# Where the value products stand and which banks they fill, in a transformer tower on one core

## The reference

```python
def _stablemax3_s(x):
    pos = 1.0 + x * (1.0 + 0.5 * x * (1.0 + x / 3.0))
    neg = 1.0 / (1.0 - x * (1.0 - 0.5 * x * (1.0 - x / 3.0)))
    return jnp.where(x >= 0, pos, neg)
# logits - max; s / sum(s)
attn = stablemax3(einsum('bhsd,bhtd->bhst', q, k) * scale)
out = einsum('bhst,bhtd->bhsd', attn, v)
h = h + out @ w_out.T + b_out
hid = relu(einsum('bsd,edf->bsef', layernorm(h), W1) + b1)
y = einsum('bsef,efd->bsed', hid, W2) + b2     # 4 experts, mixed per token
```

## Time and profile before

| | |
|---|---|
| median of 3 runs | 4353.31 us (4352.80 to 4353.53) |
| profiled execution, its own time | 4351.56 us |
| its span in the trace | 4349.7 us |
| PE busy | 4268.4 us (98%), 21312 instructions |
| DVE busy | 2292.8 us (53%) |
| ACT busy | 2174.9 us (50%) |
| HBM traffic | 14 GB/s over the span |

### The profile page before, as it was taken

One profiled execution on the slowest core, in us unless ns is written; L12 is line 12 of the kernel. 1 busy time (PEld: TensorE's weight loads), 2 busy tenths in 40 slices (PEclk: granted clock), 3 DMA queues, 4 the chain that ended last, 5 costly groups with the idle time before them and its releaser, 6 DMA issues.

```text
span 4349.7 us, 53831 instructions
## 1 busy us (share of the span) xinstructions
PE 4268.4 (98%) x21312; PEld 2342.4 (54%) x21312; DVE 2292.8 (53%) x3334; ACT 2174.9 (50%) x2945; POOL 141.4 (3%) x141
## 2 busy tenths in 40 slices
PE   6799999999999999999999999999999999999999
PEld 3455555555555555555555555555555555555555
DVE  4555555555555555555555555555555555555542
ACT  4444555445555445554455554455544555544552
POOL 1000000000000000000000000000000000000000
PEclk8899999999999999999999999999999999999999
DMA  3000000000000000000000000000000000000000
GB/s 129 12 3 14 16 16 16 16 1 16 16 16 16 3 14 16 16 16 16 1 16 16 16 16 3 14 16 16 16 16 1 16 16 16 16 3 14 4 5 8
DMA packets 29991, 65.61 MB, mean 15 GB/s; under 512 B 5360, under 2 KB 20400, under 8 KB 28720
## 3 DMA queue, kind: packets, MB, share of 16 engines
q1 hardware_dynamic: 26720, 62.07, 4.2%
q10 hardware_dynamic: 3024, 0.09, 0.0%
HBM read 49.24 MB, written 12.91 MB: 14 GB/s over the span
## 4 chain that ended last, share of the span: by engine, by line
PE 93%; DVE 4%; ACT 1%; issue 1%; POOL 0%; DMA 0%; DVEq 0%; SPq 0%; ACTq 0%; POOLq 0%
PE ps L697 32%; PE ps L708 30%; PE ps L763 6%; PE ps L732 5%; PE ps L745 4%; PE ps L720 4%; PE ps L802 4%; PE ps L811 2%; PE ps L819 2%; PE ps L687 1%; DVE probs L485 1%; DVE xn L536 1%; PE ps L788 1%; PE ps L794 1%; PE ps L776 0%
## 5 line engine op out<-in xcount | busy, mean ns | idle before, releaser
L697 PE MATMUL ps<-xn,w1s 128*128 128x394 f32 x4096 | 1562.8, 505 | 0.0
L708 PE MATMUL ps<-hT,w2s 128*128 128x394 f32 x4096 | 1535.0, 497 | 0.1
L416 ACT ACTIVATE hT<-ps,b1s 128x394 f32<-128x394 f32 x1024 | 605.3, 591 | 1400.9 <-PE ps L697 1400.9
L697 PEld LDWEIGHTS ps<-xn,w1s 128*128 128x128 f32 x4096 | 745.6, 190 | 628.4 <-issue 185.0
L708 PEld LDWEIGHTS ps<-hT,w2s 128*128 128x128 f32 x4096 | 756.1, 189 | 553.6 <-issue 35.4
L485 DVE SCALAR_TENSOR_TENSOR probs<-probs,ps 99x788 f32<-99x788 f32 x512 | 476.0, 971 | 657.5 <-ACT probs L320 657.5
L554 DVE TENSOR_REDUCE lows<-ps 99x8 f32<-99x1576 f32 x256 | 459.6, 1797 | 367.7 <-PE ps L732 367.5
L325 ACT ACTIVATE probs<-probs 99x1576 f32<-99x1576 f32 x256 | 388.4, 1517 | 194.0 <-DVE probs L485 194.0
L320 ACT ACTIVATE probs<-ps 99x788 f32<-99x788 f32 x512 | 395.5, 826 | 147.3 <-PE ps L720 145.4
L329 ACT ACTIVATE probs<-probs 99x1576 f32<-99x1576 f32 x256 | 387.1, 1512 | 0.0
L763 PE MATMUL ps<-x,wtok 128*128 128x392 f32 x744 | 256.3, 492 | 0.0
(11 more groups left out here) (82 smaller groups left out, 2502.9 us busy)
## 6 DMA issues: line engine op xcount, KB each, us to landing
x<-in_xT SPq DMA_DIRECT2D x31, 1188.0 KB, 5.6
out_rows<-rows SPq DMA_DIRECT2D x64, 99.0 KB
out_rows<-rows SPq DMA_DIRECT2D x64, 98.0 KB
w1s<-in_w SPq DMA_DIRECT2D x4, 1024.0 KB, 13.2
w2s<-in_w SPq DMA_DIRECT2D x4, 1024.0 KB, 15.1
x<-in_xT SPq DMA_DIRECT2D x6, 198.0 KB, 4.4
wtok<-in_w_tok SPq DMA_DIRECT2D x6, 128.0 KB, 3.8
wqk<-in_w_qk SPq DMA_DIRECT2D x1, 512.0 KB, 6.0
```

Source lines behind the costliest of these rows:

```text
L416: nc.scalar.activation(hT[:, j % 4, :], ps[:, U0 + j % 2, 0:N], ACT.Relu, bias=b1s[:, j // FB, j % FB:j % FB + 1]).then_inc(relu_ready, 1)
L697: ins = mm(ps[:, U0 + j % 2, 0:N], w1s[:, e, kk, f * P:(f + 1) * P], xn2[:, n % 2, kk, :], start=kk == 0, stop=kk == DK - 1)
L708: ins = mm(ps[:, Y0 + m, 0:N], w2s[:, e, f, m * P:(m + 1) * P], hT[:, j % 4, :], start=f == 0, stop=f == FB - 1)
```

## The change

1. The value products no longer have the bank `av`. `weighed(b, a)` gives them U0 or U1: each `weigh` takes one turn of the two banks of the ups. `up_turn` numbers the turns, with the four `weigh` counted in, before ups 8, 11, 15 and 19. An up whose bank was last held by a `weigh` waits for `whole` of it; the four ups right behind a `weigh` wait for the relu of the up just before them (j-1 in place of j-2).
2. `weigh` 0, 1 and 2 stand right behind score blocks 3, 5 and 7, `weigh` 3 right behind `lowest` 1. The waits of score blocks 4 and 6 and of `lowest` 0 and 2 on `whole` go, and those of `weigh` on `poly`.
3. The scalar engine's `halves` move from behind the log to between the squares and the next relu. The vector engine's `whole` moves between the two `poly` of the block, and `normal` to the end of the same block (0 from block 5 to 3, 1 from 6 to 5, 2 from behind `low` 0 and `y_added` to block 7, in front of the second `y_weighted`; 3 stays behind `whole` 3).
4. `to_rows` of the second image moves from behind `weigh` 0 to the ninth slot, two units behind `weigh` 3, and its copy on the scalar engine with it. `lowest` 2 waits for this copy in place of score block 4.

```diff
-                      low_t1=Y0, av=Y1, out0=U1, out1=Y1, mean2=U0, var2=U1, z=U0),
+                      low_t1=Y0, out0=U1, out1=Y1, mean2=U0, var2=U1, z=U0),
...
@@ -213,6 +213,18 @@
         def weight_of(e):
             return padded(w_e[:, e * 2 * GP:(e + 1) * 2 * GP])
 
+
+        UPS_BEFORE = (8, 11, 15, 19)
+
+        def up_turn(j):
+            return j + sum(j >= ups for ups in UPS_BEFORE)
+
+        def weigh_turn(a):
+            return UPS_BEFORE[a] + a
+
+        def weighed(b, a):
+            return ps[:, Y1 if b == 0 else U0 + weigh_turn(a) % 2, :]
+
...
@@ -333,9 +345,9 @@
                 img, o = a // 2, a % 2
                 act.wait_ge(av_done, at(b, 4, a + 1))
                 wait(act, out_done, at(b - 1, 2, 2))
-                nc.scalar.activation(att[:, o, img * S:(img + 1) * S], bank("av", b)[:, 0:S], ACT.Copy, scale=head_mask[:, 0:1]).then_inc(half_ready, 1)
+                nc.scalar.activation(att[:, o, img * S:(img + 1) * S], weighed(b, a)[:, 0:S], ACT.Copy, scale=head_mask[:, 0:1]).then_inc(half_ready, 1)
                 wait(act, att_ready, at(b, 4, a))
-                nc.scalar.activation(den[:], bank("av", b)[:, 0:S], ACT.Copy, scale=head_mask[:, 1:2]).then_inc(half_ready, 1)
+                nc.scalar.activation(den[:], weighed(b, a)[:, 0:S], ACT.Copy, scale=head_mask[:, 1:2]).then_inc(half_ready, 1)
 
...
                         act.wait_ge(up_done, at(n, UNITS, j + 1))
                         wait(act, down_done, at(n, UNITS, j - 3))
-                        nc.scalar.activation(hT[:, j % 4, :], ps[:, U0 + j % 2, 0:N], ACT.Relu,
+                        nc.scalar.activation(hT[:, j % 4, :], ps[:, U0 + up_turn(j) % 2, 0:N], ACT.Relu,
                                              bias=b1s[:, j // FB, j % FB:j % FB + 1]).then_inc(relu_ready, 1)
                     unit[0] += count
...
@@ -422,6 +434,8 @@
                     if has_b:
                         square(b, k, 0)
                         square(b, k, 1)
+                    if k in (3, 5, 7) and has_b:
+                        halves(b, (k - 3) // 2)
                     if k == 0 and has_n:
                         ez_of(n)
                     relus(1)
@@ -429,10 +443,8 @@
                         log_of(b, k)
                     if k in (0, 1) and has_f:
                         h_of(f, k)
-                    if k in (3, 5, 7) and has_b:
-                        halves(b, (k - 3) // 2)
-                    if k in (2, 3) and has_t:
-                        rows_of_pair(t, k - 2)
+                    if k == 2 and has_t:
+                        rows_of_pair(t, 0)
                     if k in (5, 6) and has_f:
                         q_of(f, k - 5)
                     relus(1)
@@ -443,14 +455,16 @@
                     if has_b:
                         invert(b, k)
                 for k in range(8):
+                    if k == 1 and has_b:
+                        halves(b, 3)
                     relus(1)
                     if k == 0 and has_f:
                         base_of(f, 0)
                         v_of(f, 0)
-                    if k == 1 and has_b:
-                        halves(b, 3)
                     if k == 1 and has_f:
                         base_of(f, 1)
+                    if k == 1 and has_t:
+                        rows_of_pair(t, 1)
                     if k == 2 and has_f:
                         v_of(f, 1)
                     if k < 7:
@@ -490,9 +504,9 @@
                 img, o = a // 2, a % 2
                 part = att[:, o, img * S:(img + 1) * S]
                 dve.wait_ge(half_ready, at(b, 8, 2 * a + 2))
-                nc.vector.scalar_tensor_tensor(out=part, in0=bank("av", b)[:, S:N], scalar=head_mask[:, 1:2], in1=part,
+                nc.vector.scalar_tensor_tensor(out=part, in0=weighed(b, a)[:, S:N], scalar=head_mask[:, 1:2], in1=part,
                                                op0=ALU.mult, op1=ALU.add).then_inc(whole_ready, 1)
-                nc.vector.scalar_tensor_tensor(out=den[:], in0=bank("av", b)[:, S:N], scalar=head_mask[:, 0:1], in1=den[:],
...
@@ -629,6 +643,9 @@
                         y_weighted(n, 0)
                     if has_b:
                         poly(b, k, 0)
+                    if k in (3, 5, 7) and has_b:
+                        whole(b, (k - 3) // 2)
+                    if has_b:
                         poly(b, k, 1)
                     if k == 4 and has_f:
                         spread(f, "var", var_done, vt_ready)
@@ -636,29 +653,24 @@
                         y_added(n, 0)
                     if k == 1 and has_n:
                         gates(n)
-                    if k == 5 and has_b:
-                        normal(b, 0)
-                    if k in (3, 5, 7) and has_b:
-                        whole(b, (k - 3) // 2)
                     if k == 2 and has_f:
                         centre(f)
                     if k == 4 and has_f:
                         normal_rows(f)
                     if k in (6, 7) and has_f:
                         k_of(f, k - 6)
-                    if k == 6 and has_b:
-                        normal(b, 1)
+                    if k in (3, 5, 7) and has_b:
+                        normal(b, (k - 3) // 2)
                 for k in range(8):
                     if k in (0, 4) and has_n:
                         y_weighted(n, k // 4 + 1)
                     if has_f:
                         low(f, k)
+                    if k == 1 and has_b:
+                        whole(b, 3)
                     if k in (0, 4) and has_n:
                         y_added(n, k // 4 + 1)
-                    if k == 0 and has_b:
-                        normal(b, 2)
                     if k == 1 and has_b:
-                        whole(b, 3)
...
                     pe.wait_ge(ffn_in, 16 * 2 * E)
                     pe.wait_ge(xn2_ready, at(n, 1, 1))
                     pe.wait_ge(zb_ready, at(n, 1, 1))
-                wait(pe, relu_ready, at(n, UNITS, j - 1))
+                if up_turn(j) - 2 in (weigh_turn(0), weigh_turn(1), weigh_turn(2), weigh_turn(3)):
+                    a = [weigh_turn(a) for a in range(4)].index(up_turn(j) - 2)
+                    wait(pe, relu_ready, at(n, UNITS, j))
+                    wait(pe, whole_ready, at(min(n + 1, LAST), 8, 2 * a + 2))
+                elif up_turn(j) - up_turn(j - 1) == 2:
+                    wait(pe, relu_ready, at(n, UNITS, j))
+                else:
+                    wait(pe, relu_ready, at(n, UNITS, j - 1))
                 for kk in range(DK):
-                    ins = mm(ps[:, U0 + j % 2, 0:N], w1s[:, e, kk, f * P:(f + 1) * P], xn2[:, n % 2, kk, :], start=kk == 0, stop=kk == DK - 1)
+                    ins = mm(ps[:, U0 + up_turn(j) % 2, 0:N], w1s[:, e, kk, f * P:(f + 1) * P], xn2[:, n % 2, kk, :], start=kk == 0, stop=kk == DK - 1)
                 ins.then_inc(up_done, 1)
@@ -735,6 +754,9 @@
 
             def weigh(b, a, *free):
                 img, o = a // 2, a % 2
+                if b > 0:
+                    pe.wait_ge(relu_ready, at(b - 1, UNITS, UPS_BEFORE[a] - 1))
+                wait(pe, whole_ready, at(b, 8, 2 * a))
                 pe.wait_ge(probs_ready, at(b, 8, 2 * a + 2))
...
                         for r in range(4):
-                            ins = mm(bank("av", b)[32 * r:32 * r + 32, c * S:(c + 1) * S], v[0:rows_of[half], img, half, 8 * o + 2 * r + c, :],
+                            ins = mm(weighed(b, a)[32 * r:32 * r + 32, c * S:(c + 1) * S], v[0:rows_of[half], img, half, 8 * o + 2 * r + c, :],
                                      probs[0:rows_of[half], (2 * a + half) % 4, 2 * r + 1 - c, :], start=half == 0, stop=half == 1)
                 ins.then_inc(av_done, 1)
...
@@ -953,15 +975,12 @@
 
                 if has_b:
                     gap(b, 3, read(6), *([(hc_ready, at(f, 1, 1))] if has_f else []), *([(rows_ready, at(t, 2, 1))] if has_t else []))
-                experts(2)
-                if has_b:
-                    weigh(b, 0, read(7))
-                if has_t:
-                    to_rows(t, 1, *([read(7)] if has_b else []))
+                    weigh(b, 0)
+                experts(2)
                 experts(1)
 
                 if has_b:
-                    gap(b, 4, read(8), (whole_ready, at(b, 8, 2)), *([(rows_ready, at(t, 2, 2))] if has_t else []))
+                    gap(b, 4, read(8))
                 experts(2)
                 if has_f:
                     variance(f, read(9))
@@ -969,15 +988,14 @@
 
                 if has_b:
                     gap(b, 5, read(10), *([(vt_ready, at(f, 1, 1))] if has_f else []))
-                experts(2)
-                if has_b:
-                    weigh(b, 1, read(11))
+                    weigh(b, 1)
+                experts(2)
                 if has_f:
                     project(f, "q0", 0, q_done, read(11))
                 experts(2)
 
                 if has_b:
```

(37 more changed lines are left out.)

## The result

| | before | changed | |
|---|---|---|---|
| median of 6 runs | 4352.77 us | 4319.84 us (4317.31 to 4321.28) | ratio 0.9925 [0.9913, 0.9936] |
| span of the profiled run | 4349.7 | 4318.1 | 31.6 less |
| one ordinary step (score block 0 to the next pair's) | 133.01 | 131.97 | 1.04 to 1.05 less |
| DVE / ACT busy | 2292.8 / 2174.9 | 2289.0 / 2178.8 | as before |

What follows compares the result with a forecast made beforehand. The matrix engine, busy 98% of the span, bounds the kernel. A pair saves 0.73 + 0.51 - 0.06 - 0.05 - 0.10 = 1.03 us, together 31.5 us, giving 4322 us; forecast 4312 to 4332 (0.58), range 4303 to 4344.

Steps and rivals of the forecast that it cites:

- wait of `weigh` 1: At `weigh` 1, the wait for the first half of poly 5 goes: 0.51 us a pair saved.
- switches, gross: At the four `weigh`, standing beside another small-tile block saves a way out and a way in: 0.73 us a pair.
- stall at up 8: Up 8 now waits for relu 7, behind the squares and `halves` on the scalar engine: 0.06 us lost.
- stall at variance: Variance waits for the first half of poly 4: 0.05 us lost.
- stall at project v 0: After `lowest` 0, project v 0 waits for `low` 0, delayed behind `normal` 2: 0.10 us lost.
- moved transposes: `to_rows` 1 moves to the ninth slot: 0.51 goes, 0.44 comes, the 0.07 already counted in the 0.73.
- gap beside `weigh`: Row-group score block (gap) beside column-group `weigh`: taken to cost one ordinary switch; bounds 0.19 us a place either way.
- The layout of the queues: Engine queues timed from score block 3 and `lowest` 0: stalls 0.06, 0.05, 0.10 us; margins 0.57 at down 8, 0.27 at down 16.
- A: Rival: the switch between the two tilings, score block to `weigh`, is free; about 4304 us; chance 0.10.
- B: Rival: the change saves no switches, gap to `weigh` costing what two did; 4343 us; chance 0.08.
- C: Rival: queues a quarter us later than laid out at up 8 and v 0; 4337 us; chance 0.14.
- D: Rival: slower, `normal` ahead of `y_weighted` makes the vector engine late for v 0 and down 8; 4377 us; chance 0.06.

Runs made afterwards that it cites:

- experiment 1: Kernel before with only the banks of `weigh` changed and the waits bank 0 needed removed, every order kept: 4336.41 us, a step of 132.50.
- that with no stalls: Changed kernel with relu 7 ahead of `halves` 0, `whole` behind poly's second half and `normal` 2 behind `low` 0: 4309.76 us, a step of 131.74.
- experiments 6: Changed kernel with relu 7 ahead of `halves` 0: 4332.22 us; `normal` 2 behind `low` 0: 4316.39; `whole` behind poly's second half: 4315.58; all three: 4309.76.
- experiment 3: Changed kernel with the second image's row transposes and their scalar-engine copy back in the fourth slot: 4320.51 us, a step of 132.00.
- experiment 4: Changed kernel with the products of every `weigh` issued twice: 4487.90 us; with those of every score block issued twice: 4481.36 us.
- the dose: Changed kernel with one more unneeded reciprocal on the vector engine behind each `normal`: 4346.84 us, a step of 132.87.
- that run: Kernel before with `weigh` moved directly behind its score block (3 behind `lowest` 1), bank 0 and its waits kept: 4829.59 us.

## Why the prediction was right, step by step

| term, us a pair | forecast | measured | by |
|---|---|---|---|
| wait of `weigh` 1 | 0.51 | 0.51 | experiment 1 |
| switches, gross | 0.73 | 0.76 | step of experiment 1 less that with no stalls |
| stall at up 8 | 0.06 | 0.08 | row of up 8; what experiments 6 leave |
| stall at variance | 0.05 | 0.07 to 0.08 | row; `whole` behind poly |
| stall at project v 0 | 0.10 | 0.06 to 0.08 | row; `normal` 2 late |
| moved transposes | 0 beyond the 0.07 | 0.03 more if left; not in the sum | experiment 3 |
| net | 1.03 | 1.04 to 1.05 | the steps |
| pair 1 | as the others | 1.38 | its step |
| pair 31 | 0.7 | 0.3 | from its block 0 to the end |

- **What bounds it.** "Busy hides switches" held: of 31.6 us, 17.5 are in PE's busy time, and the step lost 0.54 by neighbourhood alone (experiment 1 to the changed kernel), with no wait removed by it.
- **The unknown, gap beside `weigh`.** One ordinary switch, taken from two rows at the lower clock, was right; the repeats bear it out. The Trainium skill (TensorEngine Tiling (Array Packing), Key Properties) says that a change of tiling mode drains the engine. The times here agree, for row groups beside column groups too, with 0.17 us a change; what the engine does in that time no trace shows.
- **The layout of the queues** gave each place and each size to 0.04 us. Project v 0 was over-sized by 0.03, up 8 and variance under-sized by as much. Margins of the forecast, 0.57 at down 8 and 0.27 at down 16, were 0.64 and 0.31. Block 3 to block 5 takes 13.67 us, forecast 13.64.
- **The transposes.** Said to be free in both places, and free but for 0.03.
- **The rivals.** A and B fell by experiment 4, C (a quarter us more at up 8 and v 0) by the rows. D did not occur, but the dose shows that its price was somewhat high: the dose was worth 27 us and not 35.
- **Wrong, and small**: the wait of score block 4 on `whole` did hold somebody, once, in pair 1 (0.4 us by the row ahead of it). In pair 31 the squares start 1.33 us after score block 3, not 0.99, and up 8 stalls by 0.37, not 0.06. With the start, 0.5 us longer, and 0.02 us more saved a step, these nearly cancel, so that the span came out within 0.1 us of 4318 is in part luck; the 1.03 a step, 0.02 off, is not.
- **Left out**: the second step. I said that it keeps its order; for PE that is true, but `whole` and `normal` moved on the vector engine there too. Score block 4 came 1.1 us later against block 1 than before (18.34 for 17.21) and block 5 only 0.6 later (24.05 for 23.41). What of this is in the 0.5 us that the start lost is not told apart.

## What to carry to other kernels

Read distances between starts, not busy shares: a block of small tiles among full matmuls pays for going in and coming out, and two such blocks side by side, even of different tilings, pay one switch less. What makes such neighbours possible is a bank that the neighbour does not fill, and without it the same order costs 11%, half of it in waits and half in clock. When the bounding engine gets faster, lay out the in-order queues of the others in tenths of a microsecond around each handover, and look at who stands in front of the one that is waited for: an instruction that waits inside a chain (here `whole` between two polys) can hold the chain up for longer than it lasts: without it log 3 started 1.2 us sooner, for 0.7 us of `whole`.

## What the runs showed of the hardware

- Going from row groups of 32 to column groups of 32 costs about 0.17 us, as going to or from the full array does (0.16 to 0.18), by differences of block times in experiment 4.
- Four row groups at once take 0.67 us for 8 products of 197 fp32 columns, four column groups 1.35 for 16.
- A pause of 2.0 us of the matrix engine was followed by a stretch with a granted clock of 0.55 to 0.63; one of 3.29 us in front of `weigh` 1 in the same step was not, nor one of 2.05 in front of `weigh` 2 (1.00 behind both). The steps of that run alternate between 146.28 and 150.68 us, and in the next, longer step the same four pauses were all followed by such a stretch (0.77, 0.55, 0.56 and 0.71 over the 6 to 7.5 us behind them). What tells these pauses apart stays open.
- A wait of under 0.1 us shows in no list of waits. It is a row that is longer by as much. The lists are short of longer waits too: 0.44 for the 0.51 of `weigh` 1, 0.3 in front of variance in experiment 6, where the down ahead lasts 0.47 longer.
